# Graph attention, mixer and experts in one launch: index products settled on ScalarE, and the loads of three stages laid out anew

## The reference

```python
xn = layernorm(x)
q, k, v = xn @ Wq, xn @ Wk, xn @ Wv                   # 4 heads of 64
e = (k[src] * q[dst]).sum(-1) / 16                    # one score per edge and head
a = exp(e - segment_max(e, dst)[dst]); a = a / segment_sum(a, dst)[dst]
ft = segment_sum(v[src] * a[..., None], dst)
rst = layernorm(ft + xn) ; rst = layernorm(rst + prelu(rst @ W1 + b1) @ W2 + b2)
x = x + rst + mix(xn)       # mix: attention of 8 heads of 32 with a second-order Taylor kernel
x = x + experts(layernorm(x))                         # 8 experts 256 -> 1024 -> 256, GELU, top 2
```

## Time and profile before

| | |
|---|---|
| time, median of 3 runs | 2404.04 us (2401.11 to 2412.79) |
| the profiled execution's own time / its span | 2409.18 / 2407.3 us |
| busy: PE / DVE / ACT / POOL | 76% / 78% / 57% / 57% of the span |
| DVE in the slices of the edge stage | 9 tenths and more |
| mean granted TensorE clock | 0.862 |
| gathers L793 | 1008, 1081 ns each, 1089.7 us |
| loads `loaded<-parts` | 150 of 130 KB, 2.2 us from issue to landing |
| loads `xn_buf<-xn_dram` | 5 of 625 KB |

### The profile page before, as it was taken

One profiled execution on the slowest core, in us unless ns is written; L12 is line 12 of the kernel. 1 busy time (PEld: TensorE's weight loads), 2 busy tenths in 40 slices (PEclk: granted clock), 3 DMA queues, 4 the chain that ended last, 5 costly groups with the idle time before them and its releaser, 6 DMA issues. The chain is left out here.

```text
span 2407.3 us, 43048 instructions
## 1 busy us (share of the span) xinstructions
PE 1834.8 (76%) x12159; PEld 1279.8 (53%) x12159; DVE 1866.7 (78%) x4076; ACT 1381.1 (57%) x4345; POOL 1364.6 (57%) x1281
## 2 busy tenths in 40 slices
PE   6667777787777588787887871268899849999996
PEld 3322222332322466565665650133688739999996
DVE  6479999999999999999999998635799954444442
ACT  1246666665666376676766664459555426555553
POOL 0077777777777777777777777258100003444442
PEclk9878889888898588888878885579999969999998
DMA  8477777776777777777777777456000182222223
GB/s 235 152 216 210 214 216 210 210 214 202 214 213 211 219 209 224 221 222 229 219 223 220 225 223 222 130 163 175 23 31 30 38 300 46 36 39 35 35 38 74
DMA packets 213154, 395.07 MB, mean 164 GB/s; under 512 B 45987, under 2 KB 140274, under 8 KB 212896
## 3 DMA queue, kind: packets, MB, share of 16 engines
q0 software_dynamic: 91392, 278.99, 41.2%
q1 hardware_dynamic: 98002, 91.87, 12.8%
q10 hardware_dynamic: 23566, 22.00, 2.8%
HBM read 347.29 MB, written 48.65 MB: 164 GB/s over the span
## 5 line engine op out<-in xcount | busy, mean ns | idle before, releaser
L793 POOL DMA_INDIRECT ring<-kv_tab,idx x1008 | 1089.7, 1081 | 422.7 <-issue 413.9
L1110 ACT ACTIVATE val<-ring,val 128x64 f32<-128x64 f32 x2016 | 529.2, 336 | 79.4 <-DVE part L901 75.7
L854 DVE TENSOR_TENSOR prod<-ring,tile_bank 128x1024 f32<-128x1024 f32 x252 | 303.4, 1212 | 75.3 <-DMA ring<-kv_tab,idx 75.0
L861 DVE TENSOR_REDUCE score<-prod 128x16 f32<-128x1024 f32 x252 | 298.5, 1208 | 0.0
L2118 POOL DMA_INDIRECT x_sum<-e_yw,to_row x56 | 124.7, 2227 | 226.0 <-DVE e_yw L2144 210.5
L2103 POOL DMA_INDIRECT xr<-rows,from_row x56 | 55.6, 993 | 291.5 <-issue 287.5
L2193 PE MATMUL e_h<-e_xT,e_now 128*128 128x128 f32 x1792 | 211.2, 277 | 6.3 <-DVE e_now L2134 6.3
L2193 PEld LDWEIGHTS e_h<-e_xT,e_now 128*128 128x128 f32 x1792 | 206.4, 193 | 6.7 <-DVE e_now L2134 6.7
L2208 PE MATMUL e_yps<-e_now,e_hT 128*128 128x256 f32 x896 | 202.5, 379 | 0.0
L2158 ACT ACTIVATE e_now<-e_w_all 128x2048 f32 x56 | 106.9, 1912 | 131.0 <-PE e_yps L2208 131.0
L2208 PEld LDWEIGHTS e_yps<-e_now,e_hT 128*128 128x128 f32 x896 | 166.0, 190 | 20.3
(11 more groups left out here) (416 smaller groups left out, 4643.1 us busy)
## 6 DMA issues: line engine op xcount, KB each, us to landing
loaded<-parts SPq DMA_DIRECT2D x150, 130.0 KB, 2.2
e_w_all<-L_ffn_W SPq DMA_DIRECT2D x16, 1024.0 KB, 12.8
parts<-part ACTq DMA_DIRECT2D x126, 130.0 KB
q_win<-q_tab SPq DMA_DIRECT2D x126, 128.0 KB
ring<-kv_tab,idx POOLq DMA_INDIRECT x1008
kv_tab<-kv_t SPq DMA_DIRECT2D x25, 224.0 KB
xn_buf<-x SPq DMA_DIRECT2D x25, 125.0 KB
xn_buf<-xn_dram SPq DMA_DIRECT2D x5, 625.0 KB
```

Of the source, the lines that this page charges most:

```text
L793: pool.indirect_dma_start(out=ring[:, n % RING, e, :], out_offset=None, in_=t.kv_tab, in_offset=bass.IndirectOffsetOnAxis(ap=idx[n % 6][:, ...
L854: dve.tensor_tensor(prod[half][:, :, :], ring[:, n % RING, at, 0:F], bcast(q_ps[n % 2].unsqueeze(1), 128, L // 2, F), ALU.mult).then_inc(q ...
L861: dve.tensor_reduce(score[:, at, :], prod[half][:, :, :].rearrange("p s (h d) -> p s h d", h=HG), AX.X, ALU.add).then_inc(reduced, 1)
L1110: one = act.activation(val[n % 2][:, e, h, 0:DG], ring[:, n % RING, e, F + h * DG:F + (h + 1) * DG], ACT.Copy, scale=val[n % 2][:, e, h, D ...
```

## The change

It has four parts.

1. Settle. The four VectorE operations become five on ScalarE (two Identity/Copy, two Abs, one Relu), between `mix_first` and `mix_last` of step c = 2, ahead of weigh slot 7. PE's `find(n + AHEAD)` moves from c = 2 to c = 1 and has a fourth, one-row matmul. `times_q` and `keep_own` get a wait for `find_read`. The settle ahead of the loop is ScalarE's too.

2. Projection. x comes in six parts (tiles 0-1, 2-4, 5-9, 10-14, 15-19, 20-24): ScalarE issues the first two and then preloads the square root's table, SP issues the others between its own loads. Four groups of statistics instead of three. ScalarE stores xn. Each edge list is held once, with 8 further columns, and `parted` is called twice rather than four times; table work comes earlier by about one tile.

3. Merge. xn comes back in ten loads, rows 0 to 111 and rows 112 to 124 apart, one in every twelve steps from step 20.

4. Experts. SP first counts the four resident experts, then waits until two tiles have been turned, and only then issues the weights of experts 4 to 7.

```diff
 def stage_project(nc, a, t):
-    GROUPS = (0, 1, 3, U)
+    PARTS = (0, 2, 5, 10, 15, 20, NT)
+    GROUPS = (0, 2, 5, 15, NT)
+    NBX = NBP + 1
...
+        def load_x(eng, part):
+            at = slice(PARTS[part], PARTS[part + 1])
+            for part_rows in (slice(0, WIDE), slice(WIDE, TP)):
+                eng.dma_start(t.x_all[part_rows, at, :], a["x"].rearrange("(t p) f -> p t f", p=TP)[part_rows, at, :]
+                              ).then_inc(x_in[part], 16)
...
+            load_x(sp, 2)
...
-            for at, name, pad in zip(edges, ("src", "dst"), (1, 0)):
-                for k in range(2):
...
+            for at, name, pad, part in zip(edges, ("src", "dst"), (1, 0), (3, 4)):
...
+                load_x(sp, part)
+            load_x(sp, 5)
...
             for u in range(NT):
-                if u + 2 < NT:
-                    store_xn(u + 2)
                 sp.wait_ge(kv_ready, u + 1)
-                store(t.kv_tab, u, kv_t, kv_out)
+                store(sp, t.kv_tab, u, kv_t, kv_out)
...
-            def parted(k, i):
+            def parted(k):
...
+            stats(1)
+            spread_of(1)
+            inverse_of(1)
...
         def _(act):
-            for part in range(U):
...
+            for part in range(2):
+                load_x(act, part)
+            act.preload_act_table(ACT.Sqrt)
...
+                if u == 0:
+                    root(1)
...
+                store(act, t.xn_dram, u, xn_t, xn_out)
...
 def stage_edges_and_mix
-            def settle(n):
-
-                dve.wait_ge(found, n + 1)
-                dve.tensor_scalar(t.nneg[:, n + 1:n + 2], where_ps[n % 2][:, 2 * L:2 * L + 1], t.pcol[:, :], float(128 * n),
-                                  ALU.subtract, ALU.subtract).then_inc(placed, 1)
-                dve.tensor_copy(idx[n % 6][:, :], where_ps[n % 2][:, 0:L]).then_inc(idx_ready, 1)
-                dve.scalar_tensor_tensor(spread[n % 6][:, :], local_ps[n % 2], t.pcol[:, :], t.iota[:, :], ALU.add, ALU.is_equal
-                                         ).then_inc(spread_ready, 1)
-                dve.wait_ge(placed, n + 1)
-                dve.tensor_scalar(foreign[n % 6][:, :], where_ps[n % 2][:, L:2 * L], t.nneg[:, n + 1:n + 2], 0.0, ALU.add, ALU.not_equal
-                                  ).then_inc(find_read, 1)
             def times_q(n, half):
...
+                dve.wait_ge(find_read, min(n + AHEAD, TILES))
...
+            def settle(n):
+
+                act.wait_ge(found, n + 1)
+                act.activation(t.nneg[:, n + 1:n + 2], where_ps[n % 2][:, 2 * L:2 * L + 1], ACT.Identity, bias=less_place[:, n:n + 1]).then_inc(placed, 1)
+                act.activation(idx[n % 6][:, :], where_ps[n % 2][:, 0:L], ACT.Copy).then_inc(idx_ready, 1)
+                act.activation(gap[n % 2][:, :], local_ps[n % 2], ACT.Abs, bias=t.pcol[:, :]).then_inc(gap_ready, 1)
+                act.wait_ge(placed, n + 1)
+                act.activation(foreign[n % 6][:, :], where_ps[n % 2][:, L:2 * L], ACT.Abs, bias=t.nneg[:, n + 1:n + 2]).then_inc(find_read, 1)
+                act.wait_ge(gap_ready, n + 1)
+                act.activation(spread[n % 6][:, :], gap[n % 2][:, :], ACT.Relu, scale=-1.0, bias=t.ones[:, 0:1]).then_inc(spread_ready, 1)
...
             for n in range(TILES + 2):
                 for c in range(4):
                     mix_first(n, c)
+                    if c == 2 and n + AHEAD < TILES:
+                        settle(n + AHEAD)
...
-                pe.matmul(local_ps[n % 2], beside[:, :], later[n % 2][:, :], start=True, stop=True).then_inc(found, 1)
+                pe.matmul(local_ps[n % 2], beside[:, :], later[n % 2][:, :], start=True, stop=False)
+                pe.matmul(local_ps[n % 2], off_by[:, 0, :], off_by[:, 1, :], start=False, stop=True).then_inc(found, 1)
...
 def stage_merge
-                if n % 2:
-                    continue
-                i = (n - MR) // 2
-                if i % 2 == 0 and i < 2 * U:
-                    at = slice(i // 2 * U, (i // 2 + 1) * U)
-                    sp.dma_start(t.xn_all[:, at, :], xn_rows[:, at, :]).then_inc(f.xn_in, 16)
+                if n >= 20 and n % 12 == 8 and n < 20 + 12 * 2 * U:
+                    i = (n - 20) // 12
+                    at, part = slice(i // 2 * U, (i // 2 + 1) * U), (slice(0, WIDE), slice(WIDE, TP))[i % 2]
+                    sp.dma_start(t.xn_all[part, at, :], xn_rows[part, at, :]).then_inc(f.xn_in, 16)
...
 def stage_experts
+                for ex in range(RES):
+                    sp.wait_ge(w_in[ex], 2 * 16)
+                    sp.sem_inc(w_have, 1)
+                sp.wait_ge(turned, 2)
                 for ex in range(RES, NEX):
                     load_weights(sp, ex)
-                for ex in range(NEX):
+                for ex in range(RES, NEX):
                     sp.wait_ge(w_in[ex], 2 * 16)
                     sp.sem_inc(w_have, 1)
```

More of the change, by code:

```diff
@@ L241, in stage_project, with store @@
         block = s.block()
+        def load_x(eng, part):
[3 more added lines that the diff above has]
+                              ).then_inc(x_in[part], 16)
+        def store(eng, table, u, tile, done):
+            for part in (slice(0, WIDE), slice(WIDE, TP)):
+                eng.dma_start(table[u * TP + part.start:u * TP + part.stop, :], tile[u % R][part, :]).then_inc(done[u % R], 16)
         @block.sync
@@ L250, in _ @@
                 sp.dma_start(ap[:, :], src).then_inc(small_in, 16)
[L251 to L260 removed]
+            C = NBP * L
+            full = EDGES // C
+            for at, name, pad, part in zip(edges, ("src", "dst"), (1, 0), (3, 4)):
+                rest = EDGES - full * C
+                whole, after = (a[name][first:first + n * C].rearrange("(p c) -> p c", c=C) for first, n in ((0, full), (C, full - 1)))
+                for rows_ in (slice(0, WIDE), slice(WIDE, full)):
+                    sp.dma_start(at[rows_, 0:C], whole[rows_, :]).then_inc(edge_in, 16)
+                sp.dma_start(at[0:full - 1, C:], after[:, 0:L]).then_inc(edge_in, 16)
+                sp.dma_start(at[full - 1:full, C:], a[name][full * C:full * C + L].rearrange("(p c) -> p c", p=1)).then_inc(edge_in, 16)
+                sp.dma_start(at[full:128, 0:rest], a[name][full * C:].rearrange("(p c) -> p c", p=1)).then_inc(edge_in, 16)
+                sp.dma_start(at[full:128, rest:], a["c_tail"][pad:pad + 1, 0:NBX * L - rest]).then_inc(edge_in, 16)
+                load_x(sp, part)
+            load_x(sp, 5)
             for ap, src in ((count, a["c_count"]), (count_w, a["c_count"][0, :].partition_broadcast(NT)),
@@ L263, in _ @@
                 sp.dma_start(ap[:, :], src).then_inc(small_in, 16)
[L265 to L274, removed]
             for u in range(NT):
-                if u + 2 < NT:
-                    store_xn(u + 2)
                 sp.wait_ge(kv_ready, u + 1)
-                store(t.kv_tab, u, kv_t, kv_out)
+                store(sp, t.kv_tab, u, kv_t, kv_out)
                 sp.wait_ge(q_ready, u + 1)
-                store(t.q_tab, u, q_t, q_out)
+                store(sp, t.q_tab, u, q_t, q_out)
                 if u == 0:
@@ L706, in stage_edges_and_mix @@
         beside = s.sb("beside", [128, 128], BF16)
+        off_by, less_place = s.sb("off_by", [1, 2, 128], BF16), s.sb("less_place", [128, TILES])
+        gap = [s.sb(f"gap{i}", [128, 128]) for i in range(2)]
         spread = [s.sb(f"spread{i}", [128, 128]) for i in range(6)]
@@ L1041, in _ @@
             dve.memset(t.nneg[:, TILES + 1:], 1.0).then_inc(iotas, 1)
+            dve.memset(off_by[:, 0, :], 1.0).then_inc(iotas, 1)
+            dve.tensor_scalar(off_by[:, 1, :], t.iota[0:1, :], -1.0, None, ALU.mult).then_inc(iotas, 1)
             dve.wait_ge(c_in, 8 * 16)
-            for n in range(AHEAD):
+            dve.tensor_scalar(less_place[:, :], t.iota[:, 0:TILES], -128.0, t.pcol[:, :], ALU.mult, ALU.subtract).then_inc(places, 1)
+            for n in range(AHEAD + 1):
                 compare(n)
-                if n:
-                    settle(n - 1)
-            compare(AHEAD)
-            settle(AHEAD - 1)
             dve.tensor_copy(x.level_at[:, :].rearrange("p (j n) -> p j n", j=4), bcast(x.level_own[:, :].unsqueeze(2), 12, 4, TP)
@@ L1170, in mix_last @@
                         invert(NT - 1)
+            act.wait_ge(places, 1)
+            for n in range(AHEAD):
+                settle(n)
             for n in range(TILES + 2):
```

125 lines of the change are left out of this document (59 added, 66 removed).

## The result

| | before | changed |
|---|---|---|
| median | 2406.14 us (4 runs) | 2382.94 us (2376.96 to 2383.18, 4 runs) |
| span of the profiled execution | 2407.3 us | 2381.3 us |

The ratio is 0.9899, with a 95% interval of 0.9878 to 0.9921: 1% faster, in the forecast's range, but 23 us instead of 41. The 26.0 us between the two spans divide as follows. All boundaries are starts of GpSimd's instructions; the last gather counts with its end.

What follows compares the result with a forecast made beforehand. GpSimd's gather issue was taken to bound the edge stage. +8 (settle) - 18 (projection) - 22 (merge) - 9 (experts) = -41 us on 2409.2 gave 2368, 5 lower for the median: 2363 us, range 2325 to 2395.

Steps and rivals of the forecast that it cites:

- The bound: Edge stage: GpSimd's gather issue is the bound, not VectorE, with a floor of 10.0 us per tile of eight gathers.
- the signs named in advance: Changed trace: gather mean near 1.09 us, landing wait about 1.1 us per tile, first kv_t at 14 to 15, and others.
- Settle, +8 us: Edge stage: moving settle to ScalarE gains nothing directly, and L901, 0.59 us earlier over a gather's issue, costs 8 us.
- Rival A: Edge stage: VectorE is the bound, so settle's whole 72 us come as well, 2283 us; 7%.
- Rival B: Edge stage: ScalarE's settle delays slot 7 and the fold, which holds one more gather per tile, 90 us, 2445 us; 5%.
- Projection, -18 us: Projection: earlier first kv_t -9.3, tail -4, fewer parted calls -3.2, shorter tiles -4, queue charge +3; about -18 us.
- against it ... I charge 3: Projection: loads ahead of the first kv store on SP's queue and xn stores behind ScalarE's weight loads cost 3 us.
- Merge, -22: Merge: ten spread loads of xn hide nearly all of GpSimd's 25.4 us of waits for `loaded`; -22 us.
- Experts, -9: Experts' start: early count and a gather without weight loads beside it let e_now start at about 1969, not 1978; -9 us.
- Rival C: Loads not hidden by spreading: merge gains 10, projection 8, experts 5, edge stage loses 8; 2389 us; 15%.

Runs made afterwards that it cites:

- x3: The changed kernel with the weights of slots 0 to 3 also written to PSUM by a second exponent on ScalarE: 2316.77 us, ratio 0.9618 to before.
- x1: The changed kernel with settle back on VectorE and the edge stage as before the change: 2363.3 us, ratio 0.9808 to before.
- x8: The changed kernel with six buffers instead of three for the normalised tile: 2776.47 us, ratio 0.9866, on a chip where before took 2807.37 us.
- x10: The changed kernel with weights in PSUM, settle behind slot 7 and six xn buffers: 2791.28 us, ratio 0.9937, on a chip where before took 2806.74 us.
- x11: The changed kernel with five whole xn loads, spread, and expert weights 4 to 7 not held back: merge 136.3 us, experts 437.0 us.
- x12: The changed kernel with ten split xn loads at the old early places and all eight experts counted at the end: merge 120.3 us, experts 448.9 us.
- x7: The changed kernel with weights in PSUM, slot-innermost products and one contiguous reduction as fold: 2865.68 us, ratio 1.0221, where before took 2807.37 us.

## Why the prediction was right in its sign and off in its size

**The bound.** Right. GpSimd's row has no wait in it after the change either, 110.9 us of landing waits took up what settle freed, and x3 turned 69 us less stretch into 66 us less time. Of the signs named in advance the mean of the gathers (1093 ns), the fold's wait for ScalarE (0.23 us per tile) and e_h (7.7 us after the last routing instruction of VectorE) came; the landing wait came to 0.95 us per tile instead of 1.1, the first kv_t just after 15 us, one wait for `loaded` reached 2.4 us, and the edge stage began at 103.4 us instead of 96 to 98. The rule cited there (the Trainium skill, "SBUF — State Buffer", section "Who interferes with whom") agrees: with one operand in PSUM and the same 1.21 us, the weigh went from 67.7 us of holds to none over 30 ns.

**Settle, +8 us.** The mechanism was right: L901's counterpart lies over gathers (9.4 us more, against the 8 estimated). The size came out as +14.0: besides the 9.4, 3.3 us under other VectorE operations, nearly all the mixer's, 1.9 of longer gaps between gathers and 1.0 of holds below 30 ns, less 1.8 at L882 and L890. The own estimate of five activations at 1.2 us was near: they take 1.0 from the first start to the last end. Rival A is refuted by x1, from the other side than expected: giving the work back to VectorE made the kernel 22 us faster, up to 8 of them scatter. That the phase of the weigh against the gathers would also move, by 11 us between x1 and the changed kernel, I had left at its mean; as the same code held 66.2 us in the kernel before and 56.5 in x1, this part may be scatter, and that the forecast of +8 fell near the +14 is partly luck. Rival B, a whole gather more per tile, did not come about; its beginning did, in 27.0 us of waits for slot 7, and their own price could not be separated.

**Projection, -18 us; measured -11.2.** This is the term that was mis-sized. The start was right within about 1 us (15.28, against 14.2). From the first to the last kv_t the sum had -8.2 (-4 - 3.2 - 4 + 3); measured was +1.3 (79.9 us before, 81.1 after). The end of the stage, for which it had nothing, came 4.3 us sooner behind the last kv_t. The failing step is "against it ... I charge 3": I put the price of moving the xn stores behind ScalarE's work on the queue alone, and did not follow the buffer. The store of tile 0 starts behind `root(1)`, which waits for the second part of x; three buffers then hold `normalise(3)` for 4.72 us. The waits for these stores sum to 11.7 us, but they summed to 8.1 before, so their sum grew by only 3.6; and VectorE's waits for `kv_ps` grew from 9.0 to 13.8 us, although the sum took VectorE as what "sets the pace there". Six buffers bring back 5.7 (x8) and 4.7 us (x10) of the 9.5 missing between the first and the last kv_t. They remove the old waits with the new ones, so how much of this the move itself cost is not shown, and the rest stays open. Also, the second kv_t and not the first carries the gain on, and there it was 6.1.

**Merge, -22; measured -21.9.** The mechanism was right, and x11 and x12 show why; that the total fit so closely is in part luck. The waits for `loaded`, on which the -22 rests, gave 17.1 us (25.4 to 8.3), and another 4.2 came from GpSimd's waits for PE (18.0 to 13.8), which the sum did not have. The rule cited there (the Trainium skill, "DMA: Bandwidth & Descriptors", section "Why a DMA increments its semaphore by 16 and not by 1") agrees with the waits: whole 125-row loads 28.1 us even when spread, 112 and 13 rows 9.2 even when not. Over how many engines a load went, no row here shows.

**Experts, -9; measured -9.8.** Right. The gather's landing went from 7.2 to 2.9 us. With the early count alone (x11) the experts took 437.0 us instead of 443.0, with the weights held back as well 433.3: 6.0 us for the first and 3.7 for the second.

**Rival C** missed: the loads were hidden where it said they would not be, though by their split and not by being spread.

Of the 18 us between forecast and result 6.8 are the projection, 6.0 the edge stage and 2.8 the two stretches between stages that I had at nothing, less 0.7 that the experts gave; the rest is that the profiled difference is 26.0 and that of the medians 23.2.

## What to carry to other kernels

Where GpSimd issues gathers back to back, look first at which VectorE operations beside it read two SBUF operands: here moving one small operand to PSUM gave 66 us, and taking 72 us of work off VectorE gave a loss of 14 to 22 us. When a store moves to another queue, follow it to the buffer that it frees, and ask who fills that buffer next. An edit that buys the bound engine's time with more work and waits among the others can turn into a cost where another engine bounds: the same weights in PSUM were 2.8% faster on one chip and about 2% slower on another.

## What the runs showed of the hardware

- The kernel before took 2407 us on one chip and 2807 on two others. In the kernels profiled on those two, merge, experts and projection took what they took on the first, and the edge stage with the changed kernel's code (x8, x11, x12) 383 to 400 us more. All of that passed at the lower level of TensorE's clock (923 to 971 us of the stage against 516), with PE idle for no releaser shown; the cause is open.
- An indirect gather's issue is held by a VectorE operation with two SBUF inputs until that operation ends: over 1008 gathers by the weigh for 67.7 us, and by the same weigh of 1.21 us with one operand in PSUM (x3) for nothing.
- A VectorE reduction of 2080 elements took 3.84 us with the reduced axis at a stride of 260 elements and 2.32 with it contiguous. A product of 1024 elements written with a stride of 8 elements took 2.00 us against 1.21, and ScalarE's 128x64 weigh 397 ns against 337.
- A gather took 946 ns where nothing held it (the median of 1008 before and after). In x7, where neither the weigh nor the fold reads two SBUF operands, the mean of all 1008 is 947.
